# Edge products that stay in PSUM until their mish is done, in two stages of a graph network with experts

## The chip, the cores and the metric

The kernel runs on one core of a Trainium2 chip. The metric is the device time of one execution in microseconds. The core has five engines that each run their own stream of instructions in order: TensorE (PE) multiplies matrices and writes only PSUM, VectorE (DVE) does elementwise work and reads and writes both memories, ScalarE (ACT) does the transcendental functions, GpSimd (POOL) issues the indirect gathers, SyncE (SP) issues the plain DMAs. Engines wait for each other through semaphores.

## The reference

A graph of 6250 nodes with 256 features and 106250 edges, sorted by destination, passes four layers with residuals: a graph convolution, a mixture of six experts, an edge-conditioned aggregation, a mixture of eight experts. Two of them matter here. In short:

```python
# layer 1: graph convolution, two hops over the same edges
support = layernorm(x) @ W1                                # 128 wide
h   = relu(segment_sum(support[src] * edge_weight, dst) + b1)
out = segment_sum((h @ W2)[src] * edge_weight, dst) + b2
# layer 3: edge-conditioned aggregation
def mish(x): return x * tanh(softplus(x))
xd  = mish(layernorm(x) @ W_dense.T + b_dense)
y   = mish(edge_attr @ W_edge.T + b_edge)                  # 106250 x 256
agg = segment_sum(relu(xd[src] + y), dst)
x   = x + mish((xd + agg) @ W_out.T + b_out)
```

The edge product `mish(edge_attr @ W_edge.T + b_edge)` does not depend on the nodes.

## The kernel before

The edges are taken in groups of 512 (four chunks of 128), 208 groups with edges in them, six groups to a step, 35 steps. The stages follow each other with a barrier between them: `stage_begin` (normalisation, table of support rows), `stage_conv` (the first aggregation), `stage_mixing` (the second hop, the first experts), `stage_edges` (the edge stage), `stage_dispatch` and `stage_experts`.

The first aggregation does two things at once. For each group POOL gathers 4 x 128 rows of support by `src` into one of six slots; DVE builds one-hot masks of the destinations, scaled by the edge weight (`one_hots`); PE multiplies rows by masks into a 64-column window (`segment`, three PSUM tiles `ps`); DVE adds the window to the table of sums (`add`), which frees the slot. Beside that, four of the six edge products of a step (`KEPT`) are computed here already and stored in DRAM for the edge stage: SP loads 512 edges, PE multiplies them by the weight into one of two PSUM tiles of 128x1024 (`product`, `ps_z[r % 2]`), and the mish follows. With q = min(z, 20), the mish is z * (1 - 2/(1 + (1 + e^q)^2)). DVE adds the bias and takes the minimum (`mish_begin`, L523 and L525), ACT makes the factor with four functions in place on q (`mish_factor`, L940 to L943), and DVE multiplies (`mish_end`, L529, of negative sign). SP stores the result from `neg[r]`.

The order is written out by hand. A step has four rounds r = 0 to 3, and `BEFORE` gives each its groups: (0, 1), (2), (3, 4), (5). In round r, PE runs the round's segments and then `product(r)`, which waits for `z_free[r % 2]`. In the same round DVE runs the additions of the round's groups, in rounds 1 and 3 the masks of the next step, in round 3 also the copy of hidden rows (`rows_of`), then `mish_begin((r - 1) % 4)` and `mish_end((r - 2) % 4)`. So the mish of a product is begun one round after it and ended two rounds after it. `z_free` is given back in `mish_begin`, behind the bias addition. The function `first` (and its counterpart on PE) opens the stage with eight such rounds, in which the products run a step ahead of the segments. SP loads `edge[r]` of the next step when `mish_begin(r)` has given `edge_free`, and stores `neg[r]` when `mish_end(r)` has given `neg_ready`; `neg_out` says that the store has been done.

The edge stage gathers 256-wide node rows by POOL into six slots, adds the edge product on DVE (`message`), rectifies on ACT, multiplies by the masks on PE (`segment`) and adds into the table of sums on DVE. Groups 2 and 5 of a step (`HERE`) have their edge product computed in this stage, with one PSUM tile each (`ps_z[r]`, r = 0, 1). On PE `product(0)` comes behind the segment of group 2 and `product(1)` behind that of group 5. On DVE `mish_end(0)` stands before the message of group 2 and `mish_end(1)` before that of group 5. Besides, a slice of 180 nodes a step has its output layer and its mish computed (`output_begin`, `output_end`, L1819 to L1829).

Of the kernel before, what the change touches and what calls it, by code (L numbers as in the profile page):

```python
# [10 lines left out]
ALU = mybir.AluOpType  # L11
# [3 lines left out]
P = 128  # L15
D = 256
# [10 lines left out]
CG = 4  # L27
# [9 lines left out]
MISH = len(KEPT)  # L37
# [14 lines left out]
ZMAX = 20.0  # L52
# [41 lines left out]
def take(eng, semaphore, n=1):  # L94

    eng.wait_ge(semaphore, n)
    eng.sem_inc(semaphore, -n)  # L97


def link(eng, ins, semaphore):  # L100

    ins.then_inc(semaphore, 1)
    take(eng, semaphore)
# [309 lines left out]
def stage_conv(nc, c, table):  # L413
# [4 lines left out]
    with ExitStack() as ctx:  # L418
# [9 lines left out]
        bias = sb("bias", [P, D])  # L428
        ln2 = sb("ln2", [P, 1])
        edge = [sb(f"edge{r}", [P, KD, CG * P]) for r in range(MISH)]  # L430
        q = [sb(f"q{r}", [P, CG, D]) for r in range(MISH)]
        neg = [sb(f"neg{r}", [P, CG, D]) for r in range(MISH)]
        ps = [pb(f"ps{n}", [P, W]) for n in range(3)]
        ps_z = [pb(f"pz{r}", [P, CG, D]) for r in range(2)]
# [12 lines left out]
        own, act_own, neg_own = sem("own"), sem("act_own"), sem("neg_own")  # L447
        w_in, act_free = sem("w_in"), sem("act_free")
        per_r = lambda n: [sem(f"{n}{r}") for r in range(MISH)]
        edge_in, edge_free, z_done, z_free = per_r("edge_in"), per_r("edge_free"), per_r("z_done"), [sem(f"z_free{n}") for n in range(2)]  # L450
        z_ready, q_ready, neg_ready, neg_out = per_r("z_ready"), per_r("q_ready"), per_r("neg_ready"), per_r("neg_out")
        block = ctx.enter_context(nc.Block(no_gpsimd_drain=True))

        def load_passes(eng):
            return eng.value_load(c.passes[0:1, 0:1], min_val=1, max_val=TW // W + 1)
# [59 lines left out]
        @block.vector  # L515
        def _(dve):
            def mish_begin(r):
                take(dve, z_done[r])
                dve.sem_inc(edge_free[r], 1)

                take(dve, neg_out[r], 16)

                link(dve, nc.vector.tensor_tensor(neg[r][:], ps_z[r % 2][:], bias[:].unsqueeze(1).to_broadcast([P, CG, D]), ALU.add), neg_own)  # L523
                dve.sem_inc(z_free[r % 2], 1)
                nc.vector.tensor_scalar(q[r][:], neg[r][:], ZMAX, None, ALU.min).then_inc(z_ready[r], 1)  # L525

            def mish_end(r):
                take(dve, q_ready[r])
                link(dve, nc.vector.scalar_tensor_tensor(neg[r][:], q[r][:], -1.0, neg[r][:], ALU.add, ALU.mult), neg_own)  # L529
                dve.sem_inc(neg_ready[r], 1)  # L530

            def add(places, s):
# [111 lines left out]
        @block.tensor  # L644
        def _(pe):
            def segment(k, i, s):
                half, at = s // 3, s % 3 * CG
                if at == 0:

                    take(pe, hot_ready[half])  # L650

                take(pe, ps_free[s % 3])
                pe.wait_ge(gathered[s], k * ((IT - (s >= TAIL)) * CG * 16) + i * (CG * 16) + CG * 16)
                for j in range(CG):
                    last = pe.matmul(ps[s % 3][:], gath[s][:, j, :], hot[half][:, at + j, :], start=j == 0, stop=j == CG - 1)  # L655
                last.then_inc(ps_ready[s % 3], 1)

            def product(r):
                take(pe, edge_in[r], 16)

                take(pe, z_free[r % 2])
                for j in range(CG):
                    for m in range(KD):
                        last = pe.matmul(ps_z[r % 2][:, j, :], edge[r][:, m, j * P:(j + 1) * P], we[:, m, :], start=m == 0, stop=m == KD - 1)  # L664
                last.then_inc(z_done[r], 1)

            def turned():
                take(pe, hid_ready)
                for s in range(2):
                    last = pe.transpose(ps_t[:, s, :], hid[:, s * PART:(s + 1) * PART], c.ident[:])  # L670
                last.then_inc(turned_ready, 1)

            def step(k, i, behind):
                for r in range(MISH):
                    for s in BEFORE[r]:
                        segment(k, i, s)
                    if behind and r == 2:
                        turned()
                    product(r)

            pe.wait_ge(w_in, 32)
            with pe.Fori(0, load_passes(pe)) as k:
                for n in range(2 * MISH):
                    product(n % MISH)
                    if n < SLOTS:
                        segment(k, 0, n)
                for i in range(1, BEHIND):
                    step(k, i, False)
                with pe.Fori(BEHIND, IT - 1) as i:
                    step(k, i, True)  # L690
                for s in range(TAIL):
                    segment(k, IT - 1, s)
                for m in range(IT - 1 - BEHIND, IT):
                    turned()
# [860 lines left out]
def stage_edges(nc, c):  # L1555
# [4 lines left out]
    with ExitStack() as ctx:  # L1560
# [6 lines left out]
        we, bias, ln2 = sb("we", [P, KD, D]), sb("bias", [P, D]), sb("ln2", [P, 1])  # L1567
        neg = [sb(f"neg{r}", [P, CG, D]) for r in range(MISH)]
        edge = [sb(f"edge{r}", [P, KD, CG * P]) for r in range(MADE)]
        z, q = ([sb(f"{n}{r}", [P, CG, D]) for r in range(MADE)] for n in ("z", "q"))  # L1570
# [3 lines left out]
        xo, qo = ([sb(f"{n}{r}", [PART, 2, D]) for r in range(3)] for n in ("xo", "qo"))  # L1574
        ps_o = pb("po", [PART, 2, D])
        ps_a = [pb(f"pa{n}", [P, KD, W]) for n in range(RING)]
        ps_z = [pb(f"pz{r}", [P, CG, D]) for r in range(MADE)]
        own, act_own = sem("own"), sem("act_own")
        slot_free, w_in, consts_ready = sem("slot_free"), sem("w_in"), sem("consts_ready")
        neg_in, neg_free = each("neg_in", MISH), each("neg_free", MISH)  # L1580
        edge_in, edge_free, z_done, z_free, z_ready, q_ready = (each(n, MADE) for n in ("edge_in", "edge_free", "z_done", "z_free", "z_ready", "q_ready"))
# [198 lines left out]
        def _(dve):  # L1780
            def mish_begin(r):
                take(dve, z_done[r])
                dve.sem_inc(edge_free[r], 1)
                link(dve, nc.vector.tensor_tensor(z[r][:], ps_z[r][:], bias[:].unsqueeze(1).to_broadcast([P, CG, D]), ALU.add), own)
                dve.sem_inc(z_free[r], 1)
                nc.vector.tensor_scalar(q[r][:], z[r][:], ZMAX, None, ALU.min).then_inc(z_ready[r], 1)

            def mish_end(r):
                take(dve, q_ready[r])
                link(dve, nc.vector.scalar_tensor_tensor(z[r][:], q[r][:], -1.0, z[r][:], ALU.add, ALU.mult), own)  # L1790

            def message(k, i, s):

# [26 lines left out]
                nc.vector.tensor_scalar(qo[b][0:w, :, :], here, ZMAX, None, ALU.min).then_inc(qo_ready, 1)  # L1820

            def output_end(b=0, to=ps_o, w=PART):
                now, x = qo[b][0:w, :, :], xo[b][0:w, :, :]
                take(dve, fo_ready)
                link(dve, nc.vector.scalar_tensor_tensor(now, now, -1.0, to[0:w, 0:2, :], ALU.add, ALU.mult), own)
                if to is ps_o:
                    dve.sem_inc(o_free, 1)
                take(dve, xo_in[b], 16)
                link(dve, nc.vector.tensor_tensor(x, x, now, ALU.subtract), own)  # L1829
                dve.sem_inc(xo_ready, 1)  # L1830

            def step(k, i, places, before, begin=False, end=False):
# [442 lines left out]
```

## Time and profile before

| | us |
|---|---|
| median of 3 runs | 4281.37 |
| range of the runs | 4277.43 to 4283.28 |
| the profiled execution, first to last instruction | 4272.1 |
| PE busy in it | 3514.0 (82%) |
| POOL busy | 2823.4 (66%) |
| DVE busy | 2295.0 (54%) |
| ACT busy | 1939.7 (45%) |

Of the profiled execution the span is the only time that the profile gives. The shares are means over stages with different limits, so they say little about one stage. The first aggregation lies between 104 us, its first gather, and 1275 us; the edge stage between 2530 us, its first gather, and about 3660 us. Names in the rows are those of the program with buffer numbers left out: `conv_pz` is `ps_z` of the first aggregation, `conv_gath` its slots, `y_z`, `y_q` and `y_node` belong to the edge stage.

### The profile page before, as it was taken

What the parts mean: (1) busy time and instruction counts of PE and PEld (TensorE: products, weight loads), DVE (VectorE), ACT (ScalarE), POOL (GpSimd) and SP (SyncE); (2) the same over time, 40 slices, a digit from 0 to 9 for tenths busy, and PEclk for the clock granted to TensorE, in tenths of its full rate; (3) what the DMA queues carried; (4) which work ended last, traced back from release to release, by engine and by line L of the source; (5) the groups of instructions that cost most, each with busy time, mean ns of one, the idle gap of its engine ahead of it and who ended that gap; (6) DMA issues with size and microseconds to landing.
All of it is one profiled execution on the core that took longest, in us unless ns stands there. A gap on an engine that the chain in (4) does not pass through costs nothing. (4 is left out here: it accounts for less than half of the span.)

```text
span 4272.1 us, 68475 instructions
## 1 busy us (share of the span) xinstructions
PE 3514.0 (82%) x17723; PEld 3093.3 (72%) x17723; DVE 2295.0 (54%) x6976; ACT 1939.7 (45%) x3024; POOL 2823.4 (66%) x2732
## 2 busy tenths in 40 slices
PE   4777777777756899999999968888888888649999
PEld 4666666666645788888888867777777777538887
DVE  6566556556554445545445436666666666632222
ACT  4455555555541333333333445555555555423333
POOL 3677777777767777766676227777777777353444
PEclk7788788888776999999999987777777787559999
DMA  6455555555543222222222126666666666534443
GB/s 177 154 187 188 179 174 183 178 180 178 178 140 107 69 68 66 69 66 64 68 67 64 36 96 208 212 206 212 209 209 208 212 211 191 172 137 92 98 98 60
DMA packets 287817, 605.53 MB, mean 142 GB/s; under 512 B 61999, under 2 KB 163342, under 8 KB 287499
## 3 DMA queue, kind: packets, MB, share of 16 engines
q1 hardware_dynamic: 166267, 344.34, 25.0%
q0 software_dynamic: 114784, 245.67, 21.0%
q10 hardware_dynamic: 6576, 13.36, 0.9%
q8 instruction: 74, 1.21, 0.1%
q14 instruction: 116, 0.95, 0.1%
HBM read 460.33 MB, written 144.67 MB: 142 GB/s over the span
## 5 line engine op out<-in xcount | busy, mean ns | idle before, releaser
L1669 POOL DMA_INDIRECT y_node<-node_table,src_sb x832 | 847.6, 1019 | 379.2 <-issue 378.9
L509 POOL DMA_INDIRECT conv_gath<-support_table,src_sb x832 | 878.4, 1056 | 284.3 <-issue 259.9
L1110 POOL DMA_INDIRECT x_gath<-hidden_table,src_sb x832 | 792.9, 953 | 353.6 <-issue 259.9
L664 PE MATMUL conv_pz<-conv_we,conv_edge 128*128 128x256 f32 x2240 | 643.1, 451 | 76.9 <-PEq L97 76.7
L1682 PE MATMUL y_pa<-y_hot,y_node 128*128 128x64 f32 x3328 | 523.6, 326 | 181.7 <-PEq L97 181.1
L1682 PEld LDWEIGHTS y_pa<-y_hot,y_node 128*128 128x128 f32 x3328 | 506.8, 240 | 214.7 <-issue 212.0
L664 PEld LDWEIGHTS conv_pz<-conv_we,conv_edge 128*128 128x128 f32 x2240 | 510.2, 234 | 170.2 <-issue 81.4
L655 PE MATMUL conv_ps<-conv_hot,conv_gath 128*128 128x64 f32 x1664 | 255.6, 305 | 213.5 <-DMA conv_gath<-support_table,src_sb 210.9
L655 PEld LDWEIGHTS conv_ps<-conv_hot,conv_gath 128*128 128x128 f32 x1664 | 242.5, 219 | 245.9 <-DMA conv_gath<-support_table,src_sb 238.5
L1734 ACT ACTIVATE y_node<-y_node 128x1024 f32<-128x1024 f32 x208 | 219.4, 1056 | 340.6 <-ACTq L97 340.1
L1692 PE MATMUL y_pz<-y_we,y_edge 128*128 128x256 f32 x1104 | 361.0, 499 | 13.0 <-PEq L97 13.0
L940 ACT ACTIVATE conv_q<-conv_q 128x1024 f32<-128x1024 f32 x140 | 148.0, 1057 | 488.3 <-ACTq L97 488.3
L746 POOL DMA_INDIRECT out<-e_outs,e_node x112 | 175.0, 1562 | 281.5 <-POOLq L97 264.4
L1692 PEld LDWEIGHTS y_pz<-y_we,y_edge 128*128 128x128 f32 x1104 | 284.1, 264 | 69.2 <-issue 13.4
L1193 PE MATMUL x_ph<-x_xt,x_w 128*128 128x256 f32 (+1 forms) x1296 | 294.1, 371 | 0.5 <-PEq L97 0.3
L1199 PE MATMUL x_pm<-x_hid,x_w 128*128 128x256 f32 (+1 forms) x1296 | 289.7, 368 | 2.0 <-PEq L97 1.9
L1206 PE MATMUL x_py<-x_w,x_mid 128*128 128x256 f32 x1176 | 282.6, 381 | 1.6 <-PEq L97 1.6
L1321 ACT ACTIVATE x_hid<-x_ph,x_b 128x256 f32<-128x256 f32 (+1 forms) x324 | 129.0, 449 | 337.3 <-ACTq L97 337.0
L1127 PEld LDWEIGHTS x_ps<-x_hot,x_gath 128*128 128x128 f32 x1664 | 220.6, 201 | 74.4 <-DMA x_gath<-hidden_table,src_sb 46.3
L1804 DVE TENSOR_TENSOR y_node<-y_node,y_neg 128x256 f32<-128x256 f32 x556 | 199.7, 420 | 131.6 <-DMA y_node<-node_table,src_sb 131.6
L1127 PE MATMUL x_ps<-x_hot,x_gath 128*128 128x64 f32 x1664 | 217.9, 281 | 61.4 <-DMA x_gath<-hidden_table,src_sb 41.5
L1199 PEld LDWEIGHTS x_pm<-x_hid,x_w 128*128 128x128 f32 x1296 | 231.5, 196 | 28.7 <-issue 2.9
(256 smaller groups left out, 5844.8 us busy)
## 6 DMA issues: line engine op xcount, KB each, us to landing
conv_edge<-in_edge_t SPq DMA_DIRECT2D x140, 512.0 KB
edge_mish_table<-conv_neg SPq DMA_DIRECT2D x140, 512.0 KB
y_neg<-edge_mish_table SPq DMA_DIRECT2D x139, 512.0 KB, 4.2
y_edge<-in_edge_t SPq DMA_DIRECT2D x69, 512.0 KB
e_rows<-expert_rows SPq DMA_DIRECT2D x56, 272.0 KB, 3.3
conv_gath<-support_table,src_sb POOLq DMA_INDIRECT x832
x_gath<-hidden_table,src_sb POOLq DMA_INDIRECT x832
y_node<-node_table,src_sb POOLq DMA_INDIRECT x832, 3.1
```

Source lines behind the costliest of these rows:

```text
L509: pool.indirect_dma_start(gath[g % SLOTS][:, j, :], None, table[:, :], bass.IndirectOffsetOnAxis(ap=c.src[:, col:col + 1], axis=0),).then_ ...
L655: last = pe.matmul(ps[s % 3][:], gath[s][:, j, :], hot[half][:, at + j, :], start=j == 0, stop=j == CG - 1)
L664: last = pe.matmul(ps_z[r % 2][:, j, :], edge[r][:, m, j * P:(j + 1) * P], we[:, m, :], start=m == 0, stop=m == KD - 1)
L1110: pool.indirect_dma_start(gath[g % SLOTS][:, j, :], None, table[:, :], bass.IndirectOffsetOnAxis(ap=c.src[:, col:col + 1], axis=0),).then_ ...
L1127: last = pe.matmul(ps[n][:], gath[s][:, j, :], hot[half][:, at + j, :], start=j == 0, stop=j == CG - 1)
L1193: last = pe.matmul(ph[:, m, 0:width(u)], w_1[e][:, k, m * P:(m + 1) * P], xt[u % 2][:, k, 0:width(u)], start=k == 0, stop=k == KD - 1)
L1199: last = pe.matmul(pm[:, m, 0:width(u)], w_2[e][:, k, m * P:(m + 1) * P], hid[e % 2][:, k, 0:width(u)], start=k == 0, stop=k == KD - 1)
L1206: last = pe.matmul(py[:, s, :], mid[e % 2][:, k, s * P:(s + 1) * P], w_3[e][:, k, :], start=k == 0, stop=k == KD - 1)
L1669: pool.indirect_dma_start(node[g % SLOTS][:, j, :], None, c.t3[:, :], bass.IndirectOffsetOnAxis(ap=c.src[:, col:col + 1], axis=0),).then_i ...
L1682: last = pe.matmul(ps_a[s % RING][:, m, :], node[s][:, j, m * P:(m + 1) * P], hot[s % RING][:, j, :], start=j == 0, stop=j == CG - 1)
L1692: last = pe.matmul(ps_z[r][:, j, :], edge[r][:, m, j * P:(j + 1) * P], we[:, m, :], start=m == 0, stop=m == KD - 1)
L1734: act.activation(node[s][:], node[s][:], ACT.Relu, scale=-1.0).then_inc(msg_ready, 1)
```

## The change

The first aggregation: the bias is added in place in PSUM, the minimum reads PSUM and writes `q[r]`, and the last step of the mish reads `ps_z[r % 2]` and writes `neg[r]`. The PSUM tile is given back behind that last step, in `mish_end`; the wait for the earlier store of `neg[r]` goes to the same place. In the opening on PE the first two products come ahead, and from the third each product stands behind the segment of its round. The edge stage: the same for its two products, with the result in `z[r]`; the subtraction at the end of the output layer is split in two halves.

```diff
--- before.py
+++ after.py
@@ -515,18 +515,17 @@
         @block.vector
         def _(dve):
             def mish_begin(r):
+                here = ps_z[r % 2][:]
                 take(dve, z_done[r])
                 dve.sem_inc(edge_free[r], 1)
-
-                take(dve, neg_out[r], 16)
-
-                link(dve, nc.vector.tensor_tensor(neg[r][:], ps_z[r % 2][:], bias[:].unsqueeze(1).to_broadcast([P, CG, D]), ALU.add), neg_own)
-                dve.sem_inc(z_free[r % 2], 1)
-                nc.vector.tensor_scalar(q[r][:], neg[r][:], ZMAX, None, ALU.min).then_inc(z_ready[r], 1)
+                link(dve, nc.vector.tensor_tensor(here, here, bias[:].unsqueeze(1).to_broadcast([P, CG, D]), ALU.add), neg_own)
+                nc.vector.tensor_scalar(q[r][:], here, ZMAX, None, ALU.min).then_inc(z_ready[r], 1)
 
             def mish_end(r):
                 take(dve, q_ready[r])
-                link(dve, nc.vector.scalar_tensor_tensor(neg[r][:], q[r][:], -1.0, neg[r][:], ALU.add, ALU.mult), neg_own)
+                take(dve, neg_out[r], 16)
+                link(dve, nc.vector.scalar_tensor_tensor(neg[r][:], q[r][:], -1.0, ps_z[r % 2][:], ALU.add, ALU.mult), neg_own)
+                dve.sem_inc(z_free[r % 2], 1)
                 dve.sem_inc(neg_ready[r], 1)
 
             def add(places, s):
@@ -680,10 +679,13 @@
 
             pe.wait_ge(w_in, 32)
             with pe.Fori(0, load_passes(pe)) as k:
+                for n in range(2):
+                    product(n)
                 for n in range(2 * MISH):
-                    product(n % MISH)
                     if n < SLOTS:
                         segment(k, 0, n)
+                    if n >= 2:
+                        product(n % MISH)
                 for i in range(1, BEHIND):
                     step(k, i, False)
                 with pe.Fori(BEHIND, IT - 1) as i:
@@ -1781,13 +1783,14 @@
             def mish_begin(r):
                 take(dve, z_done[r])
                 dve.sem_inc(edge_free[r], 1)
-                link(dve, nc.vector.tensor_tensor(z[r][:], ps_z[r][:], bias[:].unsqueeze(1).to_broadcast([P, CG, D]), ALU.add), own)
-                dve.sem_inc(z_free[r], 1)
-                nc.vector.tensor_scalar(q[r][:], z[r][:], ZMAX, None, ALU.min).then_inc(z_ready[r], 1)
+                here = ps_z[r][:]
+                link(dve, nc.vector.tensor_tensor(here, here, bias[:].unsqueeze(1).to_broadcast([P, CG, D]), ALU.add), own)
+                nc.vector.tensor_scalar(q[r][:], here, ZMAX, None, ALU.min).then_inc(z_ready[r], 1)
 
             def mish_end(r):
                 take(dve, q_ready[r])
-                link(dve, nc.vector.scalar_tensor_tensor(z[r][:], q[r][:], -1.0, z[r][:], ALU.add, ALU.mult), own)
+                link(dve, nc.vector.scalar_tensor_tensor(z[r][:], q[r][:], -1.0, ps_z[r][:], ALU.add, ALU.mult), own)
+                dve.sem_inc(z_free[r], 1)
 
             def message(k, i, s):
 
@@ -1820,13 +1823,16 @@
                 nc.vector.tensor_scalar(qo[b][0:w, :, :], here, ZMAX, None, ALU.min).then_inc(qo_ready, 1)
 
             def output_end(b=0, to=ps_o, w=PART):
-                now, x = qo[b][0:w, :, :], xo[b][0:w, :, :]
+                now = qo[b][0:w, :, :]
                 take(dve, fo_ready)
                 link(dve, nc.vector.scalar_tensor_tensor(now, now, -1.0, to[0:w, 0:2, :], ALU.add, ALU.mult), own)
                 if to is ps_o:
                     dve.sem_inc(o_free, 1)
                 take(dve, xo_in[b], 16)
-                link(dve, nc.vector.tensor_tensor(x, x, now, ALU.subtract), own)
+                for half in range(2):
+                    x = xo[b][0:w, half, :]
+                    last = nc.vector.tensor_tensor(x, x, qo[b][0:w, half, :], ALU.subtract)
+                link(dve, last, own)
                 dve.sem_inc(xo_ready, 1)
 
             def step(k, i, places, before, begin=False, end=False):
```

## Rows read from the trace of the kernel before

**Rows 1.** Busy time by stretches, both stages: us, busy us (instructions), clock, DMA share, GB/s.

```profile
150.00:1240.00 1090.00, 838.20 (x3823) 718.72 (x3821) 646.57 (x1560) 593.59 (x573) 829.66 (x783) 0.83 0.55 179
2560.00:3480.00 920.00, 771.64 (x3960) 687.00 (x3960) 608.32 (x1334) 516.25 (x547) 708.54 (x695) 0.77 0.67 210
```

**Rows 2.** Groups by line: shapes, count | busy us, mean ns | idle before, releaser.

```profile
L509 POOL DMA_INDIRECT conv_gath<-support_table,src_sb x832 | 878.4, 1056 | 284.3 <-issue 259.9 <-DVEq L534 24.4
L1669 POOL DMA_INDIRECT y_node<-node_table,src_sb x832 | 847.6, 1019 | 379.2 <-issue 378.9 <-DVEq L1809 0.3
...
L529 DVE SCALAR_TENSOR_TENSOR conv_neg<-conv_q,conv_neg 128x1024 f32<-128x1024 f32 x140 | 170.5, 1218 | 2.5 <-DVEq L97 2.5
...
L525 DVE TENSOR_SCALAR conv_q<-conv_neg 128x1024 f32<-128x1024 f32 x140 | 98.8, 706 | 33.9 <-DVEq L97 33.9
...
L1790 DVE SCALAR_TENSOR_TENSOR y_z<-y_q,y_z 128x1024 f32<-128x1024 f32 x69 | 85.0, 1231 | 21.9 <-DVEq L97 21.9
...
L1786 DVE TENSOR_SCALAR y_q<-y_z 128x1024 f32<-128x1024 f32 x69 | 49.0, 710 | 16.7 <-DVEq L97 16.7
...
L1829 DVE TENSOR_TENSOR y_xo<-y_xo,y_qo 90x512 f32<-90x512 f32 (+1 forms) x35 | 24.1, 687 | 12.1 <-DVEq L97 12.1
...
L1820 DVE TENSOR_SCALAR y_qo<-y_po 90x512 f32<-90x512 f32 x33 | 22.7, 687 | 4.9
L1825 DVE SCALAR_TENSOR_TENSOR y_qo<-y_qo,y_po 90x512 f32<-90x512 f32 x33 | 22.3, 676 | 0.3 <-DVEq L97 0.3
```

**Rows 3.** List of waits: engine, line, releaser: us, times, longest.

```profile
PE conv_ps L655 <- DMA conv_gath<-support_table,src_sb: 210.9, 100, 5.0
```

**Rows 4.** Timeline, first aggregation: start us, us, engine, line [idle before].

```profile
700.76 1.22 DVE L529 SCALAR_TENSOR_TENSOR conv_neg<-conv_q,conv_neg 128x1024 f32<-128x1024 f32 x1
...
701.27 1.53 POOL L509 DMA_INDIRECT conv_gath<-support_table,src_sb  x1 [0.30 <-issue]
...
730.98 0.94 POOL L509 DMA_INDIRECT conv_gath<-support_table,src_sb  x1 [0.30 <-issue]
```

**Rows 5.** Timeline of PE alone, opening of the first aggregation.

```profile
128.60 3.69 PE L664 MATMUL conv_pz<-conv_we,conv_edge 128*128 128x256 f32 x16 [2.63 <-PEq L97]
...
138.54 6.61 PE L664 MATMUL conv_pz<-conv_we,conv_edge 128*128 128x256 f32 x16 [5.41 <-PEq L97]
144.98 1.00 PE L655 MATMUL conv_ps<-conv_hot,conv_gath 128*128 128x64 f32 x8
148.60 6.69 PE L664 MATMUL conv_pz<-conv_we,conv_edge 128*128 128x256 f32 x16 [2.62 <-PEq L97]
```

**Rows 6.** Timeline, three rounds of one step of the first aggregation.

```profile
702.51 0.22 DVE L537 TENSOR_TENSOR sums_table<-sums_table,conv_ps 128x64 f32 x1 [0.52 <-DVEq L97]
...
705.90 1.22 DVE L523 TENSOR_TENSOR conv_neg<-conv_pz,conv_bias 128x1024 f32<-128x1024 f32 x1
...
715.91 1.00 PE L655 MATMUL conv_ps<-conv_hot,conv_gath 128*128 128x64 f32 x8
...
716.75 3.67 PE L664 MATMUL conv_pz<-conv_we,conv_edge 128*128 128x256 f32 x16
...
717.23 0.22 DVE L537 TENSOR_TENSOR sums_table<-sums_table,conv_ps 128x64 f32 x1 [2.57 <-DVEq L97]
...
721.47 1.22 DVE L523 TENSOR_TENSOR conv_neg<-conv_pz,conv_bias 128x1024 f32<-128x1024 f32 x1
...
722.93 0.69 DVE L525 TENSOR_SCALAR conv_q<-conv_neg 128x1024 f32<-128x1024 f32 x1 [0.24 <-DVEq L97]
...
723.54 1.22 DVE L529 SCALAR_TENSOR_TENSOR conv_neg<-conv_q,conv_neg 128x1024 f32<-128x1024 f32 x1
...
725.14 0.33 SPq L466 DMA_DIRECT2D edge_mish_table<-conv_neg  x1
...
730.38 0.22 DVE L537 TENSOR_TENSOR sums_table<-sums_table,conv_ps 128x64 f32 x1 [0.54 <-DVEq L97]
...
731.15 1.22 DVE L523 TENSOR_TENSOR conv_neg<-conv_pz,conv_bias 128x1024 f32<-128x1024 f32 x1 [0.56 <-DVEq L97]
```

## The prediction

> **What bounds the kernel now.** I read the busy time by stretches first, then the groups of instructions by line, the list of waits, and the timeline of one step.
>
> By stretches, GpSimd (POOL) is busy 829.7 of 1090 us in the first aggregation and 708.5 of 920 us in the edge stage; TensorE (PE) is busy 838.2 and 771.6 us, at a mean granted clock of 0.83 and 0.77 of 2.4 GHz [rows 1]. PE's share is as high as POOL's, so share alone settles nothing. The groups do: POOL's gathers take 878.4 us for 832 with 259.9 us between them that wait for nothing, 1.37 us each from start to start, and it almost never waits for another engine (24.4 us in all) [rows 2]. PE waits for gathered rows, 210.9 us [rows 3]. So the gathers pace the first aggregation. A step (6 groups, 24 gathers, 4 edge products) takes 24 x 1.37 = 32.8 us, a round (a quarter of a step, one product) 8.2 us.
>
> Why a gather takes 1.056 us in the mean is in the timeline: the one during the last step of a mish (L529, two SBUF operands) takes 1.53 us, the one at 730.98 us, during the bias addition at 731.15 (L523, PSUM and SBUF), 0.94 us [rows 4, 6]. The median gather is about 0.94 us; 832 x (1.056 - 0.944) = 93 us of the first aggregation and 832 x (1.019 - 0.946) = 61 us of the edge stage are such lengthening. 0.944 and 0.946 are the undisturbed lengths that I take for the two stages; [rows 4] shows one.
>
> **The change part by part.**
>
> *VectorE's (DVE) own work.* The addition stays at 1.22 us and writes PSUM instead of SBUF. The minimum now reads PSUM: from SBUF 1024 elements take 0.706 us (L525), from PSUM 512 elements already take 0.687 us (L1820) [rows 2]. Bounds for 1024 are 0.71 and 2 x 0.69 = 1.37 us; I take 1.22, what the addition with a PSUM operand takes. The last step with one PSUM operand costs 0.676 us for 512 (L1825), against 1.218 us for 1024 (L529): no price, and I leave it at 1.22. So each mish has 0.5 us more of DVE: 18 us over the edge stage's 69, where DVE is busy 66% [rows 1] and waits for gathers hide it. Splitting the output's subtraction in two costs at most another 0.69 us for 35 (24 us, same cover) [rows 2].
>
> *POOL's gain.* Nothing in the mish then reads two SBUF operands. In the edge stage L1790 (1.23 us) and L1786 (0.71 us) run 69 times each, L1829 35 times [rows 2]. At the 0.59 us that one such last step adds to a gather [rows 4], 69 give 41 us; the other two account for up to the remaining 20 of 61 us. I take 50 us, bounds 0 (another limit stands right behind) and 61. There POOL remains the pace: a stage buffer belongs to one product per step, its mish ends before the messages of group 2 (or 5), and the next product into it comes after the segment of that same group. That wait therefore is over before PE arrives, and nothing queues behind it.
>
> *The moved release in the first aggregation.* Here two PSUM buffers serve four products of a step. Before, the addition of round r-1 frees the buffer for product(r), so PE can compute it while DVE is in round r. After, mish_end(r-2), the last thing that DVE does in round r, frees it. DVE's round r begins with the additions of the sums, which need PE's segments of round r; PE has these queued behind product(r-1). So the two engines alternate: product(r-1), segments(r), then the whole of DVE's round r, then product(r). Queued behind PE's wait are all later segments; for these DVE waits, and POOL for the slots that DVE frees. The wait for the earlier store also moves to mish_end, where the store is a whole step old; it costs nothing.
>
> DVE's part of a round, from the end of the last segment [rows 6]: start of the addition 717.23 - 716.91 = 0.32; addition 0.22; to the bias addition 731.15 - 730.60 = 0.55; bias 1.22; gap 0.24; minimum 1.22; last step 1.22, starting 0.08 before the minimum's end (723.54 against 723.62); release 725.14 - 724.76 = 0.38, read from the store that waits for the same instruction. Sum 5.29 us. Round 1 has one-hot masks: 705.90 - 702.73 = 3.17 in place of 0.55, so 7.91. Round 3 has those and the row copy: 721.47 - 717.45 = 4.02, so 8.76. A step: 2 x 5.29 + 7.91 + 8.76 = 27.3 us, with PE idle beside it. ScalarE's factor of a product starts a round earlier and is covered by PE's part.
>
> PE's part: at full clock a product is 3.67 us and a segment 1.00 us [rows 6]. PE however now pauses 5 to 9 us in each round. Where it paused 5.41 us, in the opening of this same stage, the next product took 6.61 us, and from its start to the end of one segment 144.98 + 1.00 - 138.54 = 7.44 us; after a wait of 2.62 us 6.69, though once after 2.63 us it took 3.69 [rows 5]. I take 7.44 for rounds with one segment, and 1.00 more for those with two: 2 x 7.44 + 2 x 8.44 = 31.8 us a step. The bounds are full clock throughout (3.67 + 1.00 less the 0.17 overlap = 4.5 and 5.5: 20.0 us) and half clock throughout (twice, 40 us).
>
> The step thus grows from 32.8 to 27.3 + 31.8 = 59.0 us: 26.2 us x 33 steps = 865 us. In the opening, products followed each other by 148.60 - 138.54 = 10.1 us [rows 5]; they now take some 13.1 (7.44 + 5.29, or + 7.91 in one of four), for 6 rounds: 18 us. The reordered opening issues the same products and segments and adds nothing else; its first two products start as before. The 93 us that POOL could gain in this stage are lost: POOL is late no longer, it waits for slots.
>
> Weighing the skill: the row shows 6.61 us for a product after a long pause, between the 3.67 of 2.4 GHz and twice that at 1.2 GHz [rows 5, 6]. The Trainium skill, page "TensorE: Matmul & The Clock Gate", section "HAM oscillation — how this bites in real kernels", says that a loop which waits between bursts of matmuls pays the clock's fall again in every burst. By that rule each of the 140 rounds starts at the low clock, as the sum above has it; without it the sum would be the full-clock rival below. The trace agrees in the rounds with long pauses, not in all with short ones.
>
> *Sum.* The traced execution spans 4272.1 us; the median of the runs is 4281.4, 9.3 us more, which I leave as it is. 4281.4 + 865 + 18 - 50 = 5114, rounded to 5115 us.
>
> **The rivals.**
>
> *Full clock.* Alternation as above, but PE holds 2.4 GHz. For it: product at 128.60 after a 2.63 us pause [rows 5]. Against: the new pauses are twice that. A step of 47.3 us: 14.5 x 33 = 477; 4281 + 477 - 50 = 4710 us.
>
> *Half clock throughout.* For it: bursts of 5 us between pauses of 5 to 9. Against: both slow products in [rows 5] end faster than twice 3.67. A step of 67.3 us: 34.5 x 33 + 30 = 1170; 5400 us.
>
> *Faster: the release comes before PE needs it.* The port that POOL loses to DVE is freed in both stages, and the new wait lies in the time that PE waits for gathers anyway. Then gathers run at 0.944 + 0.31 us, and the time is 4281 - 93 - 50 = 4138 us. For it: 210.9 us of such waiting [rows 3]; it decides if PE's and DVE's parts of a round fit into 24 x 1.25 / 4 = 7.5 us. Against: they add to 9.8 us even in the shortest round at full clock (4.5 + 5.29).
>
> *The port isn't freed.* If a PSUM operand doesn't help POOL, the 50 us of the edge stage go missing: 5165 us; inside the likeliest case's range.
>
> **How the numbers follow.** Alternation with slow starts 0.70 (of which 0.15 for the port not freed), full clock 0.13, half clock 0.11, the faster rival 0.04; 0.02 for something in which both cancel. Likeliest: 5115 us, its own range 4900 to 5300 (a microsecond more or less in each of 140 rounds is 140 us, the edge term 0 to 61). To hold 8 in 10 it reaches into both clock cases: 4700 to 5420. The measurement tells 0.2%, some 9 us, from no change. Faster by more 0.04, within 0.01, slower 0.95.
>
> **What would show it.** In the changed kernel, the products of the first aggregation should start right after the last step of a mish ends, with 5 to 9 us of idle PE before them; PE's granted clock there should be below 0.83; POOL should wait for DVE, for hundreds of us where it waited 24.4; the stage should be some 880 us longer, with a step of about 59 us. Gathers should average near 0.95 us, and the edge stage be some 50 us shorter at a POOL that still waits for nothing. The minimum should take about 1.22 us. I am wrong in the step itself if POOL still runs without waits in the first aggregation; wrong in the clock if the products after pauses take 3.7 or 7.3 us; wrong in the edge stage if its products wait for their buffer.

## The result, and the profile after

The changed kernel takes 4982.08 us (median of 4 runs, 4981.3 to 4983.0) against 4279.4 us for the kernel before beside it: 1.1642 times as long, 95% interval [1.1626, 1.1658]. The profiled execution spans 4981.2 us in place of 4272.1, 709.1 us more. Where they lie is seen from the first gathers of the first aggregation, the second hop and the edge stage (104.3, 1279.2 and 2530.4 us before, 106.2, 2026.0 and 3278.8 us after):

| stretch, between first gathers | before, us | after, us | difference |
|---|---|---|---|
| start to first aggregation | 104.3 | 106.2 | +1.9 |
| first aggregation | 1174.9 | 1919.8 | +744.9 |
| second hop and first experts | 1251.2 | 1252.8 | +1.6 |
| edge stage to the end | 1741.7 | 1702.4 | -39.3 |

Busy time by stretches, after (columns as in [rows 1]; the first stretch lies in the first aggregation, the second in the edge stage):

```profile
150.00:1900.00 1750.00, 908.48 (x3637) 760.17 (x3636) 688.66 (x1489) 564.97 (x545) 720.81 (x763) 0.75 0.34 107
...
3300.00:4200.00 900.00, 773.09 (x4018) 696.41 (x4019) 643.40 (x1375) 517.69 (x551) 685.15 (x706) 0.78 0.70 217
```

In the first aggregation POOL's share has gone from 76% (829.7 of 1090 us) to 41% and PE's from 77% to 52%; no engine is busy for more than 52% of the stage, as it would be if engines took turns. The granted clock fell from 0.83 to 0.75. In the edge stage PE is about as busy as before (86% against 84%) and POOL a little less (76% against 77%).

Groups by line, after, which answer to [rows 2] (L663 is the product, L521, L522 and L527 are DVE's part of the mish of the first aggregation, L97 is in the helper in which an engine waits for a semaphore):

```profile
L1671 POOL DMA_INDIRECT y_node<-node_table,src_sb x832 | 808.8, 972 | 379.2 <-issue 378.3 <-DVEq L1812 0.9
L663 PE MATMUL conv_pz<-conv_we,conv_edge 128*128 128x256 f32 x2240 | 804.1, 536 | 916.7 <-PEq L97 916.7
...
L509 POOL DMA_INDIRECT conv_gath<-support_table,src_sb x832 | 787.1, 946 | 1095.8 <-DVEq L533 874.0 <-issue 221.8
...
L521 DVE TENSOR_TENSOR conv_pz<-conv_pz,conv_bias 128x1024 f32<-128x1024 f32 x140 | 171.6, 1226 | 44.0 <-DVEq L97 44.0
...
L522 DVE TENSOR_SCALAR conv_q<-conv_pz 128x1024 f32<-128x1024 f32 x140 | 171.5, 1225 | 20.9 <-DVEq L97 0.2
...
L527 DVE SCALAR_TENSOR_TENSOR conv_neg<-conv_q,conv_pz 128x1024 f32<-128x1024 f32 x140 | 169.3, 1210 | 1.0 <-DVEq L97 1.0
```

The gathers of the first aggregation now take 0.946 us in place of 1.056, but POOL waits 874 us for DVE where it waited 24. The minimum takes 1.225 us, the last step 1.210. The gathers of the edge stage fell from 1.019 to 0.972 us. The list of waits, after (as [rows 3]), holds 139 waits of PE ahead of a product and no more wait of note for gathered rows (1.0 us in all):

```profile
PE conv_pz L663 <- PEq L97: 916.7, 139, 12.5
```

Before, PE idled 76.9 us ahead of the products. Their group in the trace of the kernel before:

```profile
L664 PE MATMUL conv_pz<-conv_we,conv_edge 128*128 128x256 f32 x2240 | 643.1, 451 | 76.9 <-PEq L97 76.7
```

One round on the timeline, after (as [rows 4, 6]):

```profile
1011.82 1.21 DVE L527 SCALAR_TENSOR_TENSOR conv_neg<-conv_q,conv_pz 128x1024 f32<-128x1024 f32 x1
...
1013.33 5.22 PE L663 MATMUL conv_pz<-conv_we,conv_edge 128*128 128x256 f32 x16 [8.58 <-PEq L97]
...
1018.39 1.89 PE L654 MATMUL conv_ps<-conv_hot,conv_gath 128*128 128x64 f32 x16
1019.72 0.22 DVE L536 TENSOR_TENSOR sums_table<-sums_table,conv_ps 128x64 f32 x1 [6.69 <-DVEq L97]
1019.81 0.94 POOL L509 DMA_INDIRECT conv_gath<-support_table,src_sb  x1 [9.93 <-DVEq L533]
...
1021.28 1.23 DVE L521 TENSOR_TENSOR conv_pz<-conv_pz,conv_bias 128x1024 f32<-128x1024 f32 x1 [0.44 <-DVEq L97]
...
1022.66 1.23 DVE L522 TENSOR_SCALAR conv_q<-conv_pz 128x1024 f32<-128x1024 f32 x1
...
1023.80 1.21 DVE L527 SCALAR_TENSOR_TENSOR conv_neg<-conv_q,conv_pz 128x1024 f32<-128x1024 f32 x1
...
1025.31 6.05 PE L663 MATMUL conv_pz<-conv_we,conv_edge 128*128 128x256 f32 x16 [5.03 <-PEq L97]
```

Read it from the top as a chain. The last step of a mish ends at 1013.03; the product starts 0.30 us later, after 8.58 us of idle PE; the two segments behind it run until 1020.28, and DVE, idle for 6.69 us, adds the first of them at 1019.72; POOL, which had waited 9.93 us for that slot, starts a gather; DVE does the bias, the minimum and the last step; and at 1025.31, 0.30 us after that, PE may go on. A whole step on PE alone, after:

```profile
1913.92 5.48 PE L663 MATMUL conv_pz<-conv_we,conv_edge 128*128 128x256 f32 x16 [7.91 <-PEq L97]
1919.24 1.90 PE L654 MATMUL conv_ps<-conv_hot,conv_gath 128*128 128x64 f32 x16
...
1926.15 6.18 PE L663 MATMUL conv_pz<-conv_we,conv_edge 128*128 128x256 f32 x16 [4.80 <-PEq L97]
1932.17 1.00 PE L654 MATMUL conv_ps<-conv_hot,conv_gath 128*128 128x64 f32 x8
1941.77 5.22 PE L663 MATMUL conv_pz<-conv_we,conv_edge 128*128 128x256 f32 x16 [8.59 <-PEq L97]
1946.82 1.90 PE L654 MATMUL conv_ps<-conv_hot,conv_gath 128*128 128x64 f32 x16
1953.74 6.04 PE L663 MATMUL conv_pz<-conv_we,conv_edge 128*128 128x256 f32 x16 [5.03 <-PEq L97]
1959.62 1.00 PE L654 MATMUL conv_ps<-conv_hot,conv_gath 128*128 128x64 f32 x8
1968.54 5.48 PE L663 MATMUL conv_pz<-conv_we,conv_edge 128*128 128x256 f32 x16 [7.91 <-PEq L97]
```

From 1913.92 to 1968.54 a step takes 54.62 us; before it took 32.8, by the pace of the gathers.

### The profile page after: what moved, and what is told of

It reads as the page before. It is cut to its first block and busy times, and to the rows that moved or that the text cites. A ratio compares the mean times of both kernels' runs of the same rounds, so it can differ in the third digit from the quotient of the medians.

```text
span 4981.2 us, 68510 instructions
## 1 busy us (share of the span) xinstructions
PE 3612.1 (73%) x17723; PEld 3164.4 (64%) x17723; DVE 2406.2 (48%) x7011; ACT 1938.1 (39%) x3024; POOL 2694.9 (54%) x2732
## 5 line engine op out<-in xcount | busy, mean ns | idle before, releaser
L663 PE MATMUL conv_pz<-conv_we,conv_edge 128*128 128x256 f32 x2240 | 804.1, 536 | 916.7 <-PEq L97 916.7
L509 POOL DMA_INDIRECT conv_gath<-support_table,src_sb x832 | 787.1, 946 | 1095.8 <-DVEq L533 874.0
L663 PEld LDWEIGHTS conv_pz<-conv_we,conv_edge 128*128 128x128 f32 x2240 | 617.6, 283 | 1070.8 <-issue 935.8
L1671 POOL DMA_INDIRECT y_node<-node_table,src_sb x832 | 808.8, 972 | 379.2 <-issue 378.3
L536 DVE TENSOR_TENSOR sums_table<-sums_table,conv_ps 128x64 f32 x208 | 46.1, 221 | 1028.9 <-DVEq L97 1028.9
L1694 PE MATMUL y_pz<-y_we,y_edge 128*128 128x256 f32 x1104 | 346.4, 483 | 11.1 <-PEq L97 11.1
L1694 PEld LDWEIGHTS y_pz<-y_we,y_edge 128*128 128x128 f32 x1104 | 273.3, 254 | 63.1 <-issue 11.5
L1208 PEld LDWEIGHTS x_py<-x_w,x_mid 128*128 128x128 f32 x1176 | 223.3, 192 | 32.0 <-issue 2.1
L1195 PEld LDWEIGHTS x_ph<-x_xt,x_w 128*128 128x128 f32 x1296 | 226.6, 196 | 22.8 <-issue 1.3
```

Source lines behind the costliest of these rows:

```text
L509: pool.indirect_dma_start(gath[g % SLOTS][:, j, :], None, table[:, :], bass.IndirectOffsetOnAxis(ap=c.src[:, col:col + 1], axis=0),).then_ ...
L1195: last = pe.matmul(ph[:, m, 0:width(u)], w_1[e][:, k, m * P:(m + 1) * P], xt[u % 2][:, k, 0:width(u)], start=k == 0, stop=k == KD - 1)
L1208: last = pe.matmul(py[:, s, :], mid[e % 2][:, k, s * P:(s + 1) * P], w_3[e][:, k, :], start=k == 0, stop=k == KD - 1)
L1671: pool.indirect_dma_start(node[g % SLOTS][:, j, :], None, c.t3[:, :], bass.IndirectOffsetOnAxis(ap=c.src[:, col:col + 1], axis=0),).then_i ...
L1694: last = pe.matmul(ps_z[r][:, j, :], edge[r][:, m, j * P:(j + 1) * P], we[:, m, :], start=m == 0, stop=m == KD - 1)
```

## The experiments

**Each half by itself.** The first run keeps the change in the edge stage only.

```diff
 stage_conv: as before the change
 stage_edges: as after the change
```

> The edge stage's part of the change alone, the first aggregation as before. Theory (the edge stage gains because the mish no longer holds up POOL's gathers, and the loss lies in the first aggregation alone): the gathers of the edge stage average 0.97 us, as in the changed kernel, and the time is 4240 us, 39 less than before. Rival (the edge stage was shorter only because the slower stages ahead of it left it in another state): 4279 us, gathers at 1.02 us.

Measured: 4233.31 us, 0.9884 of before [0.9865, 0.9903]. Groups by line of the gathers, this run:

```profile
L509 POOL DMA_INDIRECT conv_gath<-support_table,src_sb x832 | 876.3, 1053 | 281.9 <-issue 259.7 <-DVEq L534 22.2
L1669 POOL DMA_INDIRECT y_node<-node_table,src_sb x832 | 807.2, 970 | 379.3 <-issue 378.1 <-DVEq L1810 1.2
```

The edge stage's gathers are at 0.970 us, those of the first aggregation still at 1.053. So the edge stage's part is a gain of its own, and the loss lies in the first aggregation alone. The rival is out.

**The release alone.** The changed kernel with the mish of the first aggregation in SBUF again:

```diff
-link(dve, nc.vector.tensor_tensor(here, here, bias..., ALU.add), neg_own)
-nc.vector.tensor_scalar(q[r][:], here, ZMAX, None, ALU.min)...
+take(dve, neg_out[r], 16)
+link(dve, nc.vector.tensor_tensor(neg[r][:], ps_z[r % 2][:], bias..., ALU.add), neg_own)
+nc.vector.tensor_scalar(q[r][:], neg[r][:], ZMAX, None, ALU.min)...
 # mish_end reads neg[r] again; z_free stays behind it
```

> The changed kernel, but in the first aggregation the mish works in SBUF as before; only the release of the PSUM buffer stays late, in mish_end. Theory (the late release makes PE and DVE alternate, whatever memory the mish reads): the step stays above 50 us; 140 minimums are 0.52 us shorter on the path, so about 4982 - 73 = 4910 us. Rival (the operands in PSUM are what costs): back to about 4240 us.

Measured: 4971.88 us, 1.1618 of before [1.1594, 1.1641]. Groups by line, this run:

```profile
L662 PE MATMUL conv_pz<-conv_we,conv_edge 128*128 128x256 f32 x2240 | 859.9, 567 | 851.0 <-PEq L97 851.0
L509 POOL DMA_INDIRECT conv_gath<-support_table,src_sb x832 | 849.4, 1021 | 1025.3 <-DVEq L532 802.5 <-issue 222.8
```

With the operands back in SBUF the kernel is 10 us faster, of a loss of 703; the place of the release makes nearly all of it. The forecast of 4910 missed by 62 us, and the rows say where: with the shorter minimum PE waits 916.7 - 851.0 = 66 us less ahead of its products, but a product now takes 859.9 / 140 = 6.14 us in place of 804.1 / 140 = 5.74, which gives back 140 x 0.40 = 56 us. The gathers are also long again (1.021 us); PE waits for gathered rows for no more than 1.6 us in this run, so that costs nothing here.

**The order on DVE.** The changed kernel with the end of a mish right behind the additions, then the begin of the next one (in the opening too, which is left out here):

```diff
 for s in BEFORE[r]:
     add(places, s)
+mish_end((r - 2) % MISH)
+mish_begin((r - 1) % MISH)
 if behind and r == 3:
     rows_of()
 if r % 2:
     one_hots(i + 1, r // 2)
-mish_begin((r - 1) % MISH)
-mish_end((r - 2) % MISH)
```

> The changed kernel, with DVE's order within a round of the first aggregation altered: additions of the sums, then mish_end, then mish_begin, then row copy and masks. PSUM operands and the place of the release are those of the change. Theory (what counts is how much of DVE's round lies between PE's segments and the release): a round is PE's part of 4.5 to 8 us plus 0.3 + 0.2 + 0.6 + 1.2 + 0.4 = 2.7 us, or ScalarE's 4.7 us and DVE's 3.9 us, whichever is longer: 35 to 40 us a step, 4340 to 4500 us. Rival (the clock or the PSUM operands set the time, not the order): above 4850 us.

Measured: 4499.86 us, 1.0515 of before [1.0494, 1.0536], at the upper end of the forecast. The same product in two steps that follow each other, on PE's timeline of this run:

```profile
805.39 5.38 PE L661 MATMUL conv_pz<-conv_we,conv_edge 128*128 128x256 f32 x16 [3.20 <-PEq L97]
810.60 1.90 PE L652 MATMUL conv_ps<-conv_hot,conv_gath 128*128 128x64 f32 x16
...
845.18 6.44 PE L661 MATMUL conv_pz<-conv_we,conv_edge 128*128 128x256 f32 x16 [3.20 <-PEq L97]
```

The step is 39.8 us. The same instructions on the same operands, in another order, give back 482 of the 703 us. What remains shows both limits that were expected. Groups by line, and ScalarE's last function with the last step of a mish behind it on the timeline, this run:

```profile
L661 PE MATMUL conv_pz<-conv_we,conv_edge 128*128 128x256 f32 x2240 | 728.5, 497 | 507.1 <-PEq L97 507.1
...
L527 DVE SCALAR_TENSOR_TENSOR conv_neg<-conv_q,conv_pz 128x1024 f32<-128x1024 f32 x140 | 171.0, 1221 | 192.1 <-DVEq L97 192.1
```

```profile
802.46 1.15 ACT L943 ACTIVATE conv_q<-conv_q,conv_ln 128x1024 f32<-128x1024 f32 x1
...
803.87 1.22 DVE L527 SCALAR_TENSOR_TENSOR conv_neg<-conv_q,conv_pz 128x1024 f32<-128x1024 f32 x1 [1.14 <-DVEq L97]
```

DVE now idles 192 us ahead of the last step of the mish. In this step the rounds with one group wait there for ScalarE: the factor is done at 803.61, the last step starts 0.26 us later. In the rounds with two groups the first limit stands: PE's product and segments last from 805.39 until 812.50, and the next product starts 2.53 us later, at 815.03. Products still take 728.5 / 140 = 5.20 us.

**The clock.** Two runs fill PE's waits with matmuls of constants, ahead of each product in the steps; the first with small ones, the second with ones of the products' shape (and `ps` widened to hold them). Their results are overwritten by the segments (which then skip the wait that `filler` has done; left out here).

```diff
+def filler(s, amount):
+    take(pe, ps_free[s % 3])
+    for n in range(amount):
+        pe.matmul(ps[s % 3][:], we[:, 0, 0:P], we[:, 1, 0:W], start=True, stop=True)
 # second run: 9 or 15 of pe.matmul(ps[s % 3][:, 0:D], we[:, 0, 0:P], we[:, 1, :], ...)
...
+filler(BEFORE[(r + 1) % MISH][0], (16, 28)[r % 2])
 product(r)
```

> The changed kernel, with 16 (rounds 0 and 2) or 28 (rounds 1 and 3) extra small matmuls of constants before each product of the first aggregation's steps; their results are overwritten. PE so works in most of its wait. Theory (a product takes 5.7 us in the mean because each follows a pause, at a lower granted clock): products near 3.7 us, 2 us less in each of 132 rounds, about 4980 - 270 = 4710 us, if the extra matmuls end before the release; the waits for the release stay. Rival (the product is long for another reason, such as the PSUM traffic of DVE): products at 5.7 us and 4980 us or more.

Measured: 4894.46 us, 1.1437 of before [1.1414, 1.146]: between theory and rival. The product's group in this run:

```profile
L665 PE MATMUL conv_pz<-conv_we,conv_edge 128*128 128x256 f32 x2240 | 713.1, 488 | 269.8 <-PEq L98 269.8
```

> The changed kernel, with 9 (rounds 0 and 2) or 15 (rounds 1 and 3) extra matmuls of the products' own shape before each product of the first aggregation's steps, of constants and overwritten later; some 4 and 7 us at full clock, in waits of 5 and 8. Theory (the clock of a product follows what PE did before it, and the small matmuls of the earlier run only partly stood in for products): products near 3.7 us, a step some 8 us shorter than 54.6, about 4710 us; PE still waits for the release in each round. Rival (something else than the clock makes the product long): products at 5 us or more, 4890 us or more.

Measured: 4750.85 us, 1.1115 of before [1.1094, 1.1135]. The product's group, and three products that follow each other on PE's timeline, two with the fillers ahead of them, of this run:

```profile
L665 PE MATMUL conv_pz<-conv_we,conv_edge 128*128 128x256 f32 x2240 | 569.1, 412 | 230.4 <-PEq L98 225.4 <-issue 5.0
```

```profile
809.19 5.38 PE L665 MATMUL conv_pz<-conv_we,conv_edge 128*128 128x256 f32 x16 [2.05 <-PEq L98]
...
816.14 4.10 PE L677 MATMUL conv_ps<-conv_we 128*128 128x256 f32 x18
821.34 3.69 PE L665 MATMUL conv_pz<-conv_we,conv_edge 128*128 128x256 f32 x16 [1.09 <-PEq L98]
...
825.70 6.69 PE L677 MATMUL conv_ps<-conv_we 128*128 128x256 f32 x30
833.78 3.69 PE L665 MATMUL conv_pz<-conv_we,conv_edge 128*128 128x256 f32 x16 [1.39 <-PEq L98]
```

Small matmuls brought the product from 5.74 to 5.09 us, matmuls like its own to 4.07 (569.1 / 140), with most at 3.69 us, the length at full clock, and some longer, such as the 5.38 us at 809.19. The second run is 231 us faster than the changed kernel, and 140 x (5.74 - 4.07) = 234 us is what the products gave. So the first aggregation's loss has two terms: some 230 us for the clock, and the rest, 4751 - 4233 = 518 us against the run with the edge stage's part alone, for taking turns at nearly full clock. (Products were not at full clock in the kernel before either: 643.1 / 140 = 4.59 us.)

The granted clock says the same. Two products of the changed kernel, as stretches (columns as in [rows 1]; a clock of 1 is 2.4 GHz, of 0.5 1.2 GHz, and these means lie between the two):

```profile
1013.33:1018.55 5.22, 5.22 (x18) 4.33 (x19) 0.00 (x0) 3.46 (x4) 0.00 (x0) 0.70 0.66 219
1025.31:1031.36 6.05, 6.05 (x18) 4.95 (x19) 0.00 (x0) 3.13 (x3) 3.27 (x4) 0.61 0.70 223
```

Length times granted clock is 5.22 x 0.70 = 3.65 and 6.05 x 0.61 = 3.69 us, what a product takes at full clock. So the lower clock is all that lengthens these two, and the rival (the PSUM traffic of DVE) is out for them.

**What is left of POOL's delays.** These runs keep the edge stage's part and look for a gain in the first aggregation without the late release. First the last step of the mish in four instructions, in SBUF:

```diff
-link(dve, nc.vector.scalar_tensor_tensor(neg[r][:], q[r][:], -1.0, neg[r][:], ALU.add, ALU.mult), neg_own)
+for j in range(CG):
+    last = nc.vector.scalar_tensor_tensor(neg[r][:, j, :], q[r][:, j, :], -1.0, neg[r][:, j, :], ALU.add, ALU.mult)
+link(dve, last, neg_own)
```

> The edge stage of the change, the first aggregation as before but with the last step of the mish in four instructions of 256 elements. Theory (a gather waits while one instruction with two SBUF operands runs, so that short ones cost it less): gathers of the first aggregation average about 0.98 in place of 1.05 us, 832 x 0.07 = 60 us off the 4233 of the edge stage's part alone: 4175 us. DVE's extra 0.45 us for each of 140 mish steps lies in its waits. Rival (what counts is the total time of two-operand work): gathers at 1.05 us or more, 4233 us or above.

Measured: 4198.14 us, 0.9822 of before [0.9808, 0.9835], below the edge stage's part alone by more than both intervals. A minimum and the gather that meets it, the four pieces and a gather that meets these alone, on this run's timeline, and the gathers as a group:

```profile
705.52 0.69 DVE L525 TENSOR_SCALAR conv_q<-conv_neg 128x1024 f32<-128x1024 f32 x1 [0.24 <-DVEq L97]
...
705.63 1.40 POOL L509 DMA_INDIRECT conv_gath<-support_table,src_sb  x1 [0.30 <-issue]
...
714.50 1.42 DVE L530 SCALAR_TENSOR_TENSOR conv_neg<-conv_q,conv_neg 128x256 f32<-128x256 f32 x4
...
715.01 1.06 POOL L509 DMA_INDIRECT conv_gath<-support_table,src_sb  x1 [0.30 <-issue]
```

```profile
L509 POOL DMA_INDIRECT conv_gath<-support_table,src_sb x832 | 832.2, 1000 | 284.5 <-issue 253.5 <-DVEq L536 31.0
```

Under the four pieces this gather takes 1.06 us; under the one instruction it took 1.53 [rows 4]. Both start 0.51 us after the instruction or the first piece. Over the stage, counted on the timelines, the 134 gathers that start under pieces, clear of a minimum, take 1.05 us in the mean and 1.07 at most; before, the 137 that likewise start under the one instruction took 1.34 and 1.53. So what counts is the length of one instruction, and the rival is out. The mean of all gathers fell to 1.000, not to 0.98, and the time by 35 us, not 60: the gather that meets the minimum (705.52) still takes 1.40, and POOL's waits grew from 22.2 to 31.0 us. PE now idles 274.9 us for its PSUM tile, 76.7 before, where it had waited for gathered rows.

> As the run before, with the minimum in four instructions too. Theory: what is left of lengthened gathers in the first aggregation is the minimum's (up to 0.26 us each in the trace), so the mean gather falls to about 0.96 us and the time to 4160 us. Rival (DVE's added fixed costs, some 0.4 us a mish, put the mish on the path): no better than the run before.

```diff
-nc.vector.tensor_scalar(q[r][:], neg[r][:], ZMAX, None, ALU.min).then_inc(z_ready[r], 1)
+for j in range(CG):
+    last = nc.vector.tensor_scalar(q[r][:, j, :], neg[r][:, j, :], ZMAX, None, ALU.min)
+last.then_inc(z_ready[r], 1)
```

Measured: 4229.25 us, 0.9892 of before [0.9876, 0.9907]: slower than with the minimum whole. Groups by line, this run:

```profile
L509 POOL DMA_INDIRECT conv_gath<-support_table,src_sb x832 | 816.4, 981 | 328.1 <-issue 251.9 <-DVEq L538 76.1
...
L526 DVE TENSOR_SCALAR conv_q<-conv_neg 128x256 f32<-128x256 f32 x560 | 136.5, 306 | 33.8 <-DVEq L97 33.8
```

The gathers are shorter again, 0.981 us, yet POOL waits 76 us for slots, and PE 303.8 us for its PSUM tile. The theory of gathers alone fails here, and the rival holds: DVE's minimum now takes 136.5 / 140 = 0.98 us in place of 0.71. That it hurts by putting the next release later is the theory of the last run below.

> The edge stage's part alone, with the subtraction at the end of the output layer in one piece as before. Theory (the two halves hold up POOL less than the one): up to 0.4 us for each of 35, so gathers of the edge stage at 0.98 in place of 0.97 us and 4240 us. Rival (they make no difference): 0.97 us and 4233 us.

```diff
-for half in range(2):
-    x = xo[b][0:w, half, :]
-    last = nc.vector.tensor_tensor(x, x, qo[b][0:w, half, :], ALU.subtract)
-link(dve, last, own)
+x = xo[b][0:w, :, :]
+link(dve, nc.vector.tensor_tensor(x, x, now, ALU.subtract), own)
```

Measured: 4236.78 us, 0.9912 of before [0.9894, 0.993]; gathers at 0.974 us against 0.970. The intervals of this run and of the edge stage's part overlap: whether the split subtraction is worth anything stays open.

The last two put the masks and the row copy behind the mish in the kernel's own order, with the early release (in the opening too, which is left out here):

```diff
 for s in BEFORE[r]:
     add(places, s)
+mish_begin((r - 1) % MISH)
+mish_end((r - 2) % MISH)
 if behind and r == 3:
     rows_of()
 if r % 2:
     one_hots(i + 1, r // 2)
-mish_begin((r - 1) % MISH)
-mish_end((r - 2) % MISH)
```

> The version with the edge stage's part and the last step of the mish in four pieces, and in DVE's rounds of the first aggregation the mish now comes ahead of the row copy and the masks. Theory (what lies on DVE between PE's segments and the release counts, in the kernel before too, as soon as the gathers stop being the last to arrive): the release comes some 3 us sooner in two of four rounds, POOL's 31 us of waits for slots go, gathers pace the stage at 1.00 us: 4198 - 30 = 4168 us. Rival (the mish, earlier in the round, waits for ScalarE instead): 4198 us or more.

Measured: 4178.61 us, 0.9758 of before [0.9745, 0.9771], 11 us above the forecast and below the run without the new order by more than both intervals. Its gathers:

```profile
L509 POOL DMA_INDIRECT conv_gath<-support_table,src_sb x832 | 833.8, 1002 | 277.9 <-issue 257.3 <-DVEq L536 20.6
```

The gain is not where it was forecast: POOL's waits fell by 10 us, not by 31. From the stage's first gather to its last the trace is 5 us shorter than without the new order (1101.6 in place of 1106.6), from the last gather to the first of the next stage 9 us (21.8 in place of 30.7). PE's wait for its PSUM tile fell from 274.9 to 69.7 us; it waits for gathered rows again (209.8 us; 210.9 in [rows 3]).

> The same order with the minimum in four pieces too. Theory: the minimum in pieces lost because it put the release later, not because of POOL (gathers were shorter, 0.98 us, and POOL waited 76 us for slots); with the masks behind the mish those waits go, and the time is that of 0.98 us gathers: about 15 us below the run with the minimum whole, some 4150 us. Rival (four pieces cost DVE too much whatever the order): slower than the run with the minimum whole.

Measured: 4162.9 us, 0.9727 of before [0.9714, 0.9741], 13 us above the forecast. Its gathers:

```profile
L509 POOL DMA_INDIRECT conv_gath<-support_table,src_sb x832 | 804.1, 966 | 279.0 <-issue 258.0 <-DVEq L538 20.9
```

With this order POOL's waits stay at 21 us and the pieces pay: the minimum in pieces, which cost 31 us in the old order, now gains 16. The last version beats both kernels, by 117 us against before. It has the edge stage of the change, and in the first aggregation the release where it was.

## Why the prediction was right

It said 5115 us, slower, with 4700 to 5420 as its range; 4982 lies in it, and also in the likeliest case's 4900 to 5300.

- *The turns.* As forecast, products start right behind the last step of a mish, PE idles 5 to 9 us ahead of each, and POOL waits for hundreds of microseconds (874). The run with the release alone shows that the late release is the cause; the run with another order on DVE shows that its place behind DVE's round makes 482 of the 703 us.
- *DVE's part of a step.* Forecast 27.3 us; measured 54.62 less PE's four parts of 7.22, 7.02, 6.95 and 6.88 us, read from the step above as product start to segment end, which leaves 26.6. In the round from 1013.33 the gap between bias and minimum is 0.15 us where 0.24 was taken, and PE goes on 0.30 us behind the last step where 0.38 was taken; four times both are the 0.7 us.
- *PE's part.* The term that was mis-sized. Forecast 2 x 7.44 + 2 x 8.44 = 31.8 us; measured 28.1. In rounds with one segment the product took 6.0 to 6.2 us where 6.6 were taken from the stage's opening; in those with two, after the longest pauses, 5.2 to 5.5. 3.7 us, with the 0.7 of DVE's part, over 33 steps are 145 us, and the first aggregation lost 745 us in place of 865 + 18 = 883. The opening's 13.1 us a round should have been 13.4 by its own terms, 2 us more in all.
- *The clock.* Slow starts were the right case among the three: 5.74 us a product, between 3.67 and twice that. The Trainium skill, page "TensorE: Matmul & The Clock Gate", section "HAM oscillation — how this bites in real kernels", has bursts between waits pay the fall of the clock each time. The trace agrees for every product of the step above (5.22 to 6.18 us). The run filled with products shows the price, 230 us. The full-clock rival's 4710 us was near the 4751 of that run.
- *The minimum.* Taken at 1.22 us, measured 1.225. For the edge stage the sum was wrong: 0.5 us for each of 69 is 35 us, not 18. DVE's waits hid it all the same, since POOL kept the pace (it waited 0.9 us for DVE there).
- *The edge stage.* Forecast 50 us, bounds 0 and 61. The stretch from its first gather is 39 us shorter in the trace, and its gathers shrank by 832 x (1.019 - 0.972) = 39 us; the medians of the part alone give 47. Its products did not wait: PE idled 11.1 us ahead of them, in sum, before 13.0. What was missed is that the messages' additions, with two operands in SBUF, lengthen gathers too: 832 x (0.972 - 0.946) = 22 us are left, and the 220 gathers that start under such an addition make 18 of them, counted on the timeline, after:

```profile
3707.56 1.43 DVE L1807 TENSOR_TENSOR y_node<-y_node,y_neg 128x256 f32<-128x256 f32 x4 [2.93 <-DMA y_node<-node_table,src_sb]
3707.62 1.19 POOL L1671 DMA_INDIRECT y_node<-node_table,src_sb  x1 [0.31 <-issue]
```

- *The port.* The rival that PSUM operands don't help POOL is out in both stages: 0.946 us in the first aggregation, against 1.021 in the run with the same late release and operands in SBUF, and 0.972 us in the edge stage, against 1.019.
- *The rival that went the other way* (the wait hidden in PE's waits for gathers) failed on the sum that was held against it; even the shortest round of the step above is 1953.74 - 1941.77 = 12.0 us, where 7.5 was the point from which it decides.

## What to carry to other kernels

Before a buffer's release is moved to a later instruction, write down what its engine has queued ahead of that instruction, and whether any of it needs the engine that waits for the buffer: if so, with too few buffers the two take turns. The edge stage has the same late release but a buffer of its own for each product of a step, and PE idled 11 us there; a third buffer for the four products of the first aggregation was not tried. Give back a scarce buffer as early in an in-order round as its use allows, and put work that nobody waits for, such as masks for the next step, behind it. An operand moved to PSUM, or an instruction cut in pieces, shortened the gathers that VectorE's long instructions on SBUF had held up. The pieces need no buffer to be held, but they take VectorE longer (1.42 us in place of 1.22, 0.98 in place of 0.71), and the minimum in pieces lost 31 us until masks and row copy stood behind the mish.

## What was unexpected of the hardware

After longer pauses the products were shorter: 5.2 to 5.5 us behind 7.9 to 8.6 us of idle, 6.0 to 6.2 behind 4.8 to 5.0, in a step that repeats. And a shorter pause can give back most of what it saves: with 0.5 us less of DVE's work in each round PE waited 66 us less, but the product grew from 5.74 to 6.14 us, 56 us in all. The granted clock was 0.70 in a product of the one kind and 0.61 in one of the other. Why it rises earlier in the one is open; no run told it apart.

A GpSimd gather's delay is not proportional to VectorE's work: one instruction of 1.22 us with two SBUF operands lengthened a gather to 1.53 us, four with 1.42 us in all to 1.06. The Trainium skill, page "SBUF — State Buffer", section "SBUF: two separate sides", says that such an instruction, against a GpSimd operation that reads SBUF, holds a port that the two engines share until it ends, and the other blocks. Both rows fit that: the gathers grew by 0.59 and 0.12 us, where 0.71 us of the one instruction were left when the gather started, and a piece lasts 0.42 in the mean.
